# Moving the next layer's keys, its values and the first layer's norm between stages of a four-layer decoder kernel

## The reference, cut to what matters

```
x = x + tanh(g_xattn[0]) * _L0_xattn_ref(_layernorm(x), ctx, bias, ...)   # 16 heads of 8, then a norm, a gelu layer 128-512-128, a norm
x = x + tanh(g_ffn[0])   * _L0_ffn_ref(_layernorm(x), Wr, W1, W3, W2)     # top 2 of 8 experts, capacity 640, silu gate
x = x + tanh(g_xattn[1]) * _L1_xattn_ref(_layernorm(x), ctx, ctx, mask, W_Q, W_K, W_V, W_O)   # 16 heads of 64
    # scores = (x W_Q)(ctx W_K)^T, out = softmax(scores) (ctx W_V) W_O
```

## Time and profile before

| | us |
|---|---|
| runs (3), median | 1314.72 |
| lowest and highest | 1314.2, 1321.32 |
| profiled execution, its own time | 1319.26 |
| its span, first to last instruction | 1317.1 |
| busy in the span: PE, DVE | 1079.0, 702.6 |
| busy in the span: ACT, POOL | 599.8, 480.8 |
| attention L0 ends, lead begins | 150 |
| experts' PE work | 234.8 to 349.6 |
| wide attention begins, its first scores | 375.1, 389.1 |

### The profile page before, as it was taken

One profiled execution on the slowest core, in us unless ns is written; L12 is line 12 of the kernel. 1 busy time (PEld: TensorE's weight loads), 2 busy tenths in 40 slices (PEclk: granted clock), 3 DMA queues, 4 the chain that ended last, 5 costly groups with the idle time before them and its releaser, 6 DMA issues. The chain is left out here.

```text
span 1317.1 us, 26494 instructions
## 1 busy us (share of the span) xinstructions
PE 1079.0 (82%) x8602; PEld 748.6 (57%) x8602; DVE 702.6 (53%) x3348; ACT 599.8 (46%) x1507; POOL 480.8 (37%) x728
## 2 busy tenths in 40 slices
PE   6999691899989999989896778894778999962883
PEld 4777461677735666664343665884643444542773
DVE  7666474233368676644464642112747888755012
ACT  3544451333369766624221432332562666631553
POOL 4767427143307555522004554442020000067343
PEclk8999795899989999999997965998785999985887
DMA  9789701231169970010750022654041222005533
GB/s 246 228 220 172 192 13 51 80 98 46 50 96 121 161 111 2 1 37 27 150 101 1 3 97 85 174 170 126 2 144 37 66 59 71 26 18 165 145 91 101
DMA packets 154055, 124.60 MB, mean 95 GB/s; under 512 B 14042, under 2 KB 132202, under 8 KB 153929
## 3 DMA queue, kind: packets, MB, share of 16 engines
q1 hardware_dynamic: 139704, 106.77, 35.9%
q0 software_dynamic: 7168, 12.83, 3.0%
q10 hardware_dynamic: 7056, 3.42, 1.0%
HBM read 88.12 MB, written 37.70 MB: 96 GB/s over the span
## 5 line engine op out<-in xcount | busy, mean ns | idle before, releaser
L957 ACT ACTIVATE L_Z<-L_Z,L_nmx 128x154 f32<-128x154 f32 x256 | 105.1, 414 | 42.1 <-DVE L_nmx L1007 41.9
L3424 DVE CUSTOM_DVE_ANT_0 L3s_masked<-L3s_psS,L3s_trilw 128x512 f32<-128x512 f32 (+3 forms) x256 | 109.7, 486 | 24.0 <-PE L3s_psS L3251 23.5
L321 POOL TENSOR_TENSOR L_Z<-L_Z,L_mx 128x512 f32<-128x512 f32 x84 | 87.4, 1041 | 65.6 <-DVE L_mx L691 62.1
L3379 ACT ACTIVATE L3s_E<-L3s_psT 128x512 f32<-128x512 f32 (+1 forms) x192 | 87.7, 530 | 49.3 <-PE L3s_psT L3264 49.0
L826 POOL TENSOR_TENSOR L_Z<-L_Z,L_rin 128x488 f32<-128x488 f32 x64 | 63.9, 999 | 110.9 <-DVE L_rin L1015 110.9
L868 PE MATMUL L_psS<-L1k_G,L_xnT 128*128 128x462 f32 x192 | 82.4, 525 | 2.8 <-DVE L_nmx L1007 1.4
L691 DVE CUSTOM_DVE_ANT_0 L_Z<-L_psS,L_Z 128x154 f32<-128x154 f32 x256 | 63.4, 313 | 33.8 <-PE L_psS L377 31.7
L1007 DVE CUSTOM_DVE_ANT_0 L_Z<-L_psS,L_mask 128x154 f32<-128x154 f32 x256 | 67.7, 313 | 11.4 <-PE L_psS L868 10.8
L552 ACT ACTIVATE L_E<-L_psT 128x512 f32<-128x512 f32 x84 | 46.4, 596 | 56.1 <-PE L_psT L390 56.1
L1025 DVE COPY L_PT<-L_psT 122x512 f32<-122x512 f32 x64 | 43.6, 682 | 40.4 <-PE L_psT L878 39.6
L2468 DVE TENSOR_TENSOR L0f_h<-L0f_h,L0f_psB 128x384 f32<-128x384 f32 (+1 forms) x64 | 31.2, 487 | 62.3 <-PE L0f_psB L2430 58.5
(11 more groups left out here) (617 smaller groups left out, 2818.3 us busy)
## 6 DMA issues: line engine op xcount, KB each, us to landing
L_Z<-in_fside_Bx16xSxS SPq DMA_DIRECT2D x16, 1232.0 KB, 7.4
L2f_w<-in_L_ffn_W SPq DMA_DIRECT2D x39, 256.0 KB, 2.8
slotsL<-empty SPq DMA_DIRECT2D x1, 8320.5 KB, 76.2
L1m_cb<-comb_rows SPq DMA_DIRECT2D x8, 1024.0 KB, 10.0
L3f_w<-in_L_ffn_fc_w SPq DMA_DIRECT2D x32, 256.0 KB, 3.8
L0f_w<-in_L_ffn_W SPq DMA_DIRECT2D x24, 256.0 KB, 4.4
L3s_QS<-q_parts SPq DMA_DIRECT2D x144, 32.0 KB
L3s_KS<-k_parts SPq DMA_DIRECT2D x48, 96.0 KB
```

The costliest lines, as they stand in the source:

```text
L321: nc.gpsimd.tensor_tensor(Z[:, t % NZ, h, 0:KM_], Z[:, t % NZ, h, 0:KM_], top.broadcast_to([P, HG, KM_]), ALU.subtract).then_inc(z_ready, 1)
L957: last = nc.scalar.activation(Z[:, t % 2, h], Z[:, t % 2, h], ACT.Exp, scale=-1.0, bias=nmx[:, t % 2, h:h + 1], accum_out=sums[:, t % 2, h ...
L3379: nc.scalar.activation(E[:, g.par, h, EO[group[0]]:EO[group[0]] + wd], psT[:, k, 0:wd], ACT.Exp).then_inc(t_free, 1)
L3424: last = nc.vector.tensor_tensor_reduce(masked[:, k, at:at + wd], psS[:, k, at:at + wd], trilw[:, S - wd:S], 1.0, LOW, ALU.add, ALU.max, m ...
```

## The change

Four things are moved. Nothing is computed otherwise.

1. **The lead's weights.** SP issues w1, b1 and w2 in the attention, behind the clear of the table, and waits for them before it leaves the block. The lead no longer waits for them.
2. **The lead's norm.** DVE's aggregates follow each tile in the attention's loop (`gather`). ACT takes the roots of the first 12 tiles in the attention, behind the last exponentials, and DVE normalises these 12 tiles around the last residuals (`normalise_next`). The lead does the last four only. ACT also calls a gelu on one element early.
3. **The keys** move from behind the experts into the lead's tail, as 16 units (j, half of the batches) on other banks (psT's first for the keys, psA and psY for G). PE's, ACT's and DVE's streams interleave the units with the route of groups 2 and 3. ACT evicts both heads of units 0 to 9; from unit 10 on DVE takes one of them, behind `place(3)`. `place(2)` stands ahead of `second(3)` on DVE now. The first 3 units stand ahead of `positions(2)` on PE, units 0 to 9 ahead of `positions(3)`.
4. **The values** move from the start of wide attention to the end of the experts' block (`Values1`), ahead of the collect on PE, ACT and DVE. The collect's loads go into the two halves of `pay` instead of XN and XT. In wide attention DVE builds the mask after the first normalisation.

The diff, cut to its core:

```diff
--- before.py
+++ after.py
@@ quad_attention, SP
-            sp.wait_ge(m.rest_loaded, 16 * len(m.later))
+            for dst, src in c["ahead"]:
+                sp.dma_start(dst, src).then_inc(m.rest_loaded, 16)
+            sp.wait_ge(m.rest_loaded, 16 * (len(m.later) + len(c["ahead"])))
@@ quad_attention, ACT, behind exponentials(t, 4)
+                if not late and t == NTL - 1:
+                    for n in range(TB - 1):
+                        ts = slice(n * TB, (n + 1) * TB)
+                        act.wait_ge(mv1_ready, ts.stop)
+                        nc.scalar.activation(std1[:, ts], m.mv1[:, ts, 1], ACT.Sqrt, bias=m.const["eps"]).then_inc(std1_ready, 1)
@@ quad_attention, DVE, behind divide(t - 2)
+                if not late and 0 <= t - 3:
+                    gather(t - 3)
+                if not late and t >= NTL:
+                    normalise_next(t - NTL)
...
             if not late:
                 measure(NTL - 1)
-                own.wait()
-                for t in range(NTL):
-                    own.done(nc.vector.bn_aggr(m.mv1[:, t], m.st1[:, t]))
+                normalise_next(2)
+                gather(NTL - 1)
@@ Lead0.tensor
-        for k in (2, 3):
-            route.turn(pe, k)
-            route.logits(pe, k)
-            route.positions(pe, k)
+        route.turn(pe, 2)
+        pe.wait_ge(self.t1_done, TB)
+        keys.keys(pe, 0)
+        route.logits(pe, 2)
+        pe.wait_ge(self.h_free, 4 * TB)
+        pe.wait_ge(self.o_free, TB)
+        key_units(0, 3)
+        route.positions(pe, 2)
+        key_units(3, 7)
+        route.turn(pe, 3)
+        key_units(7, 8)
+        route.logits(pe, 3)
+        key_units(8, 10)
+        route.positions(pe, 3)
+        key_units(10, keys.UNITS)
@@ Lead0.scalar
+        nc.scalar.activation(self.std[:, 0:1], m.const["eps"], ACT.Gelu)
...
+        route.turned_rows(act, 2)
+        keys.keep_keys(act, 0)
+        route.turned_copies(act, 2)
         deviation2(3)
-        route.turned_rows(act, 2)
-        route.turned_copies(act, 2)
+        key_units(0, 5)
         route.deviation(act, 3)
+        key_units(5, 7)
         route.turned_rows(act, 3)
+        key_units(7, 8)
         route.turned_copies(act, 3)
+        key_units(8, keys.UNITS)
         route.exponentials(act)
@@ Lead0.vector
+            if k == TB - 1:
+                route.place(k - 1)
             second(k)
             route.moments(k, m.X)
-            if k >= 1:
+            if 1 <= k < TB - 1:
                 route.place(k - 1)
...
         route.place(TB - 1)
+        for u in range(self.keys.SHARED, self.keys.UNITS):
+            self.keys.vector(dve, u)
         route.shares()
@@ Keys1, the new units
+    def keys(self, pe, u):
+        j, f = divmod(u, 2)
...
+        if u >= 1:
+            pe.wait_ge(self.k_done, u)
+        pe.matmul(self.k_bank[:, 0:2 * S2], self.wk[:, j * P:(j + 1) * P], ctx_all[:, f * 2 * S2:(f + 1) * 2 * S2],
+                  start=True, stop=True).then_inc(self.k_full, 1)
+
+    def weights(self, pe, u):
+        j = u // 2
+        pe.wait_ge(self.k_done, u + 1)
+        if u >= 2:
+            self.evicted(pe, u - 2)
...
+    def tensor(self, pe, u):
+        if u + 1 < self.UNITS:
+            self.keys(pe, u + 1)
+        self.weights(pe, u)
...
+    def scalar(self, act, u):
+        if u + 1 < self.UNITS:
+            self.keep_keys(act, u + 1)
+        act.wait_ge(self.g_full, u + 1)
+        self.nc.scalar.copy(*self.place(u, 0)).then_inc(self.g_done0, 1)
+        if u < self.SHARED:
+            self.nc.scalar.copy(*self.place(u, 1)).then_inc(self.g_done1, 1)
@@ routed_experts
+        back = (m.XN, m.XT3) if ends else (pay[:, 0, :, 0:D], pay[:, 1, :, 0:D])
...
-            collect.second(act, keys)
+            if values is not None:
+                values.scalar(act)
+            collect.second(act)
...
-            if keys is not None:
-                keys.tensor(pe)
+            if values is not None:
+                values.tensor(pe)
...
-            collect.add(dve, keys)
+            if values is not None:
+                values.vector(dve)
+            collect.add(dve)
```

More of the change, by code:

```diff
@@ L733, in measure, with gather, normalise_next @@
                 own.done(nc.vector.bn_stats(m.st1[:, t], m.X1[:, t]))
+            def gather(t):
+                own.wait()
+                nc.vector.bn_aggr(m.mv1[:, t], m.st1[:, t]).then_inc(mv1_ready, 1)
+            def normalise_next(n):
+                ts = slice(n * TB, (n + 1) * TB)
+                dve.wait_ge(std1_ready, n + 1)
+                own.done(nc.vector.reciprocal(r1[:, ts], std1[:, ts]))
+                own.wait()
+                for t in range(n * TB, (n + 1) * TB):
+                    nc.vector.tensor_scalar(m.XN[:, t], m.X1[:, t], m.mv1[:, t, 0:1], r1[:, t:t + 1], ALU.subtract, ALU.mult)
             for t in range(-1, NTL + 2):
@@ L834, in _ @@
         def _(pe):
[L835 to L846, removed]
-                                     start=True, stop=True, skip_group_check=True)
-                last.then_inc(r_in, 1)
-            pe.wait_ge(v_out, 2 * B)
-            pe.wait_ge(r_out, B)
             def turn_x(u):
@@ L990, in _ @@
             normalise(0)
-            for b in range(B):
-                dve.wait_ge(r_in, b + 1)
-                nc.vector.tensor_copy(Vr[:, b], r_bank[b % 2][:, 0:256]).then_inc(r_out, 1)
+            own.done(nc.vector.tensor_copy(mask[:], m.maski[:]))
+            own.wait()
+            own.done(nc.vector.tensor_scalar(mask[:], mask[:], 0.0, -MASKED, ALU.is_equal, ALU.mult))
+            own.wait()
             def reduce(t, g):
@@ L1828, in outputs, with key_units @@
                     pe.wait_ge(self.o_free, k - 1)
[L1829 to L1834 removed]
+            o = self.psY[:, k % 2, i * P:(i + 1) * P]
+            for j in range(4):
+                last = pe.matmul(o, self.h[:, k % 2, j, i * P:(i + 1) * P], self.w2[:, j], start=(i == 0 and j == 0),
+                                 stop=(i == TB - 1 and j == 3), skip_group_check=True)
+            if i == TB - 1:
                 last.then_inc(self.o_full, 1)
+        keys = self.keys
+        def key_units(lo, hi):
+            for u in range(lo, hi):
+                keys.tensor(pe, u)
         turn1(0)
@@ new lines, in keys @@
+    def keys(self, pe, u):
+        j, f = divmod(u, 2)
+        ctx_all = self.m.ctxT[:].rearrange("p b k -> p (b k)")
+        if u >= 1:
[7 more added lines that the diff above has]
+            self.evicted(pe, u - 2)
+        for b in range(2):
+            for a in range(2):
+                last = pe.matmul(self.g_banks[u % 2][:, a, b * S2:(b + 1) * S2], self.wq[64 * a:64 * a + 64, j],
+                                 self.KT[64 * a:64 * a + 64, u % 2, b * S2:(b + 1) * S2], start=(b == 0), stop=(b == 1),
+                                 skip_group_check=True)
+        last.then_inc(self.g_full, 1)
@@ L2227, in first, with second @@
             sp.wait_ge(self.stored, 16 * TB)
-    def second(self, act, keys=None):
-        m = self.m
-        if keys is not None:
-            for j in range(TB):
-                keys.scalar(act, j)
+    def second(self, act):
+        m, back = self.m, self.back[1]
         for p in range(2):
@@ L2316, in routed_experts @@
         route = lead.route
-        if keys is not None:
-            keys.open(sb, sem, psT, (psA, psB))
-        collect = Collect(nc, sem, m, c["key"], route.shared, c.get("out"))
+        back = (m.XN, m.XT3) if ends else (pay[:, 0, :, 0:D], pay[:, 1, :, 0:D])
+        collect = Collect(nc, sem, m, c["key"], route.shared, back, c.get("out"))
+        values = None if ends else Values1(nc, sem, m, c["wv"], [psA[:, 0], psA[:, 1], psB[:, 0], psB[:, 1]], [psT[:, 0], psT[:, 1]])
         block = ctx.enter_context(nc.Block())
```

234 lines of the change are left out of this document (106 added, 128 removed).

## The result

The changed kernel takes 1303.61 us (median of 4 runs, 1302.37 to 1307.38) where the kernel before takes 1315.65 (4 runs, the three of the first table and one more): a ratio of 0.989, 95% interval 0.985 to 0.993, 12.0 us less. The forecast was 1302.7. The two spans, 1317.1 and 1305.3, differ by 11.8.

A forecast was written before the change was run, and what follows sets the result against it. POOL's 32 scatters bound the lead's tail, then the untouched experts, then full ACT in wide attention. Experts' start 2.0, collect 4.3 and wide attention's start 5.7 sum to 12.0 us off 1314.72: 1302.7, range 1297 to 1309.

The forecast's parts named there:

- Leaving the attention: End of the attention: stage ends 0.5 to 1.1 us later, 0.6 taken; the moved weights' loads cost nothing.
- The lead's start: Lead up to the first scatter: outputs and first scatter (188.51 to 184.5) come 4.0 us earlier, bounds 2.7 and 4.8.
- The tail: Scatters of groups 2 and 3: key units ahead of the route give half back; experts start 2.0 us earlier.
- rival 1: Lead's tail: units warm PE's clock, POOL has no wait; 5.3 us instead of 2.0, time 1299.4; chance 0.17.
- rival 2: Lead's tail: units hold the route longer, low clock or waits; lead 0 to -7.3, 1304.7 to 1312; chance 0.17.
- as the clock comes back: Step in the lead's tail: units 0 and 1 at 2.6 us, unit 2 at 1.4, positions of group 2 at 204.7.
- The experts: Stage behind the lead's tail: the change does not touch it, so it got no term of its own.
- The collect: From the experts' end E to the last sum: E + 20.7 instead of E + 25.1, 4.3 us taken, bounds 3 and 5.5.
- the landing: In the collect: 3.2 us from ACT's issue of its loads to its first scaling, at E + 13.3.
- Wide attention's start: First scores after the stage's start: 7.3 us earlier less 1.6 for cold PE, 5.7 earlier, bounds 4.0 and 7.3.
- The cold scores: Wide attention's first scores at the low clock: first exponentials 0.9 us later, a second gap of 0.7, together 1.6.

The follow-up runs named there:

- the series: Follow-up kernels run on three chips of the same kind, where the kernel before takes 1341, 1347 and 1343 us; the unedited change has ratio 0.997 there.
- One queue: The change with all eight loads of the experts' results issued by SP, instead of four on SP and four on ACT; ratio 0.995 to the kernel before.
- the warm runs: The change with matmuls without use added, 16 behind the units and 6 at wide attention's start, or 18 behind the values and 8 there; ratios 1.009 and 1.004.

## Why the prediction was right, and where it was off

- **Leaving the attention**, predicted 0.6 later: 2.3 at the last copy, 2.4 at the stage's end. The norm's operations behind the last copy cost 0.1 net, less than said. The 2.2 us lie in the tile in which PE stalls under the clear. I priced the loads behind it at nothing since the DMA engines were empty from 145 on; they are in early enough, but with them in the queue this tile is 1.5 us longer in the mean of eight traces, which is less than their spread. That the clear itself stalls PE is shown by moving it away. Through what it does was not tested. One candidate is the loading of instructions, which the profile lists as a DMA queue of its own: one packet of it falls between 126 and 130 us and takes 2.1 us of a DMA engine in the result's trace, 1.4 in the kernel before and 1.2 with the clear moved away.
- **The lead's start**, 4.0 us earlier: the first scatter 2.8 earlier. From the attention's last copy on it is 5.1, where I had 4.6; the attention's end, 1.7 later than said, takes more than that back. No table load stood before the first root, as assumed.
- **The tail**, 2.0 given back: 0.1 gained. The clock stayed full, so positions came 1 us earlier than walked (215.4 for 216.5), and POOL waited 1.0 us. That is between the forecast and rival 1. On the three chips of the experiments it was rival 2: the units at the low clock and 11 us given back, more than its bound of 7.3 later than now. The walk's step that depended on luck is "as the clock comes back", and in the result's trace the luck was good: I gave the low clock two units. In the change's trace of the series it took six of the sixteen, on top of ACT's late starts.
- **The experts**, said to be untouched: 1.4 given back. They start at the low clock in both; before, it rose 2.9 us after their first hidden matmul (237.72, 240.6), after the change 5.4 us (234.99, 240.4), at nearly the same time of the program. Half of the 2.5 us more at the low clock is 1.25, nearly all of the 1.4. In the ten traces of the change and its variants where nothing stands in front of the experts the time from their load to E lies between 118.2 and 119.4, in the two of the kernel before it is 118.0 and 118.5: chance more than a cost.
- **The collect**, 4.3 less: 3.0. The queue was right (issue at E + 9.4, said 10.1; from the first scaling to the end 7.4, as said); the mis-sized term is the landing, 5.3 us for 3.2. ACT's 1 MB now follows SP's by 2 us instead of 4.5, which is the likely cause, though not the whole rule: with the values back in wide attention both queues issue at once, and the first rows come 4.4 us behind. One queue gives 2.5 us back.
- **Wide attention's start**, 5.7: 6.2 in the result, 5.4 to 5.5 in the series. The cold scores cost 0.9 to 1.5 us (said 1.6), shown by the warm runs. By the Trainium skill ("TensorE: Matmul & The Clock Gate", Part 1) activity releases the throttled clock; the trace agrees, 4.9 us for ten records at the full clock, behind the values or behind matmuls without use, and 6.05 here behind an idle PE.

The sum was right by luck in its terms: 1.7 us lost at the attention, 1.4 at the experts and 1.3 in the collect were met by 2.1 more in the tail, 0.5 each in the lead's start and the wide stage, and 1.2 behind it: the errors of the terms, up to 2.1 us each, are larger than that of the sum. The mechanisms of three of the four parts were right; that the keys cost the tail nothing held in the result's trace alone.

## What to carry to other kernels

Work moved into the idle time of an in-order engine is free only at the clock that the engine then has: price it at both levels, and ask whether the chain that shares the engine can stand the higher price. A large transfer in flight can stall an engine that doesn't wait for it (3.5 us here); put it where no full pipeline runs, and look at what is queued behind it. Loads that one stage consumes in pairs go on one queue, in the order of their use, where that gained 2.5 us here.

## What the runs showed of the hardware

- While the 2.58 MB clear, read from one small tile, is in flight, PE stands 1.5 to 2.1 us without a releaser and one tile of the attention is 9.4 us long instead of 5.9 (means of four traces and of two). With the three loads queued behind it PE stands 1.5 to 5.1 us and the tile is 7.9 to 14.2 long.
- PE's clock at the start of the experts rose 2.9 us after the first hidden matmul in one execution and 5.4 in another, and was full throughout behind 15 us of matmuls without use. In the tail an idle time of 0.40 us left it full, and in the trace with 2.12 us it was low for the next 10 us.
- The same kernel differs by 2% between the result's runs and the three chips (1315 and 1341 to 1347 us), and in the two traces of it the difference is no common factor: it lies in the stretches where POOL scatters beside the other engines, with hand-offs from PE to ACT and DVE 2 to 10 us late. The change gained 12 us in the one setting and nothing that could be measured in the other.
- A kernel run against itself had a ratio of 0.997 with an interval of 0.995 to 1.000.
